# Routing in two halves with 0/1 products for the first expert, and half of the cross-attention's queries made inside its loop

## The chip, the cores and the metric

The kernel runs on one core of a Trainium2 chip, as a program of five engines with queues of their own: TensorE (PE: matmuls and transposes into the 8 banks of PSUM, `ps`), VectorE (DVE), ScalarE (ACT), GpSimd (POOL) and SyncE (SP, which issues most transfers). They are ordered by semaphores alone. The metric is the device time of one execution in microseconds (us).

## What is computed

Sixteen sequences of 64 tokens (T = 1024, width D = 512) pass three blocks, each added to its input after a layer norm. With B = 16, S = 64, NT = 8 tiles of 128 tokens, DC = 4 chunks of 128 features:

```python
x = x + xattn(norm(x), ctx)      # self-attention, cross-attention on 1601 context rows each, MLP of 512
x = x + recurrent(norm(x))       # gates, convolution, linear recurrence of width 768
h = norm(x)                      # then a mixture of 8 experts, 2 for each token, 160 places each
logits = h @ gate_w.T; probs = softmax(logits); top_p, top_i = top_k(probs, 2)
w = top_p / (sum(top_p) + 1e-9)
my_rank = place of the token in the expert's queue (a running count over all tokens)
keep = my_rank < capacity
out = x + sum over the kept (token, expert): w * (silu(h @ Wg[e].T) * (h @ Wu[e].T)) @ Wd[e].T
```

In the cross-attention the keys' matrix is folded into the queries: `m2 = Wq2 @ Wk2.T`, `q = h @ m2` (512 wide), and the scores are `q @ ctx.T`, so that each sequence needs its context twice: by columns (`ctxT`, 3.2 MB) for the scores, and by rows (`ctx`, 3.2 MB) for the values.

## The kernel before

**Order of the dense work.** `dense_groups()` lists every product or transpose that takes a whole PSUM bank; group g has bank g % 8, and it waits until the group 8 places before it has been copied out (`wait_bank_free`). On each engine instructions run in the order written.

**Into the cross-attention.** PE makes the self-attention's `z`, then `m2`, then for each half h of the tokens the four transposes `t1` of its tiles and the four products `q` of 512 columns. ACT copies them out (`hT`, `qT`). DVE meanwhile adds the residual and normalises the eight tiles, computes a decay constant in some 23 tiny steps on 128x6 values (`lac`), waits for all eight `q` copies and clears a piece of PSUM (`pad_cleared`), on which the first scores wait.

**The cross-attention's loop**, for n = 0 to 16 on PE: `scores(n)` (32 matmuls, L508), `transpose_probabilities(n - 1)`, `transpose_output(n - 2)`, `exchange(n)` (tiny products with the counts that DVE made from the scores), `values(n - 1)` (26 matmuls, L532 and L534). Scores of n + 1 need `shifted` of DVE. SP loads the context through two buffers each for columns and rows: the columns of n + 1 once `scores(n - 1)` are done, then the rows of n once `values(n - 2)` are done, in this one order. After the loop come the MLP and the recurrent block, bound to PE.

**Into the experts.** The last dense product `wo` (18 matmuls for a tile) gives the residual; DVE's `residual`, `norm_stats` and `norm_apply` with POOL's `norm_scale` make `hr`, the normalised rows. PE transposes all eight tiles (`t5`) and multiplies them by the gate's weights (`logits`, 8 columns); then, as one chain, DVE makes softmax, top 2 and one-hot (`oh`), PE counts ranks (`rk`), and DVE makes the indices (`scat`). POOL scatters the rows to HBM (`xs`) with 16 indirect transfers, SP waits for all of them and loads the rows of experts 0 and 1 back (`xe`), PE transposes those of expert 0 (`transpose_slots`), and ACT and DVE split them into high and low parts (`xsplit`).

```python
sp.wait_ge(scattered, 16 * NT * TOPK)
load_rows(0, 0)
load_rows(1, 1)
for f in range(RING, FC):
    load_unit(0, f)
```

**The experts.** Each runs 8 units f of weights (768 KB, in a ring of 4, three split ahead): `gate_up` (24 matmuls of 320 columns, L743) and `down` (8 of 512, L759). ACT and DVE split the weights and the hidden values. POOL stores the results, and after the last expert gathers them by `gath` and DVE mixes them in with the routing weights.

## Time and profile before

| | |
|---|---|
| Time, median of 3 runs | 1165.77 us (1164.29 to 1166.39) |
| Profiled execution | 1166.8 us; its span, first to last instruction, 1165.0 us |
| Busy over the span | PE 88%, DVE 49%, ACT 33%, POOL 16% |
| Mean granted TensorE clock | 0.945 |
| Into the cross-attention: first scores start | 150.63 us |
| Cross-attention: last values start | 393.77 us |
| Last `wo` done, first `gate_up` starts | 709.85 us, 773.15 us |

Times in views count from the span's start. A busy PE in a view is modelled from pipelined matmuls, so the pace of a group is read from starts, not from durations. "Idle before" is how long the engine stood before the instruction, with what released it. The clock is 1.00 at 2.4 GHz and 0.50 at 1.2 GHz.

### The profile page before, as it was taken

To read this page: it belongs to the slowest core of one execution; us is meant where nothing else is said; L and a number is where in the kernel's file an instruction comes from. 1 tells how busy PE (TensorE), PEld (TensorE's weight loads), DVE (VectorE), ACT (ScalarE), POOL (GpSimd) and SP (SyncE) were. 2 spreads that over 40 slices of the span, in tenths; PEclk is the share of its full clock that TensorE was granted. 3 is DMA by queue.
4 is the path that set the end of the run, shared out by engine and by line. 5 is a ranking of instruction groups with operands and counts; after the bars stand their busy time and mean duration, and the time that the engine had idled before them with its cause. 6 is when DMAs were issued, how large, how long until landed. Compare 5 with 4: busy or idle time off the path is not lost.

```text
span 1165.0 us, 13668 instructions
## 1 busy us (share of the span) xinstructions
PE 1030.0 (88%) x5132; PEld 760.6 (65%) x5132; DVE 565.7 (49%) x1081; ACT 382.6 (33%) x598; POOL 184.4 (16%) x174
## 2 busy tenths in 40 slices
PE   6999989999988899777999998159999999999970
PEld 3454434444433487665888887159999999999970
DVE  3046523333223287593446664325655655565534
ACT  1211211211111323124566632024444444444420
POOL 2002400000000156243512121500000000000005
PEclk9999999999999999898999997569999999999995
DMA  9724059999999511011411102354545545534306
GB/s 322 320 113 201 25 198 393 418 401 400 401 409 404 204 59 55 1 54 58 129 55 33 35 1 109 117 178 161 184 156 186 180 142 186 195 135 158 131 23 216
DMA packets 38867, 208.04 MB, mean 179 GB/s; under 512 B 5264, under 2 KB 6672, under 8 KB 34592
## 3 DMA queue, kind: packets, MB, share of 16 engines
q1 hardware_dynamic: 33424, 188.47, 43.9%
q0 software_dynamic: 5392, 18.88, 4.6%
q8 instruction: 33, 0.54, 0.2%
q14 instruction: 18, 0.15, 0.0%
HBM read 190.56 MB, written 16.78 MB: 178 GB/s over the span
## 4 chain that ended last, share of the span: by engine, by line
PE 71%; DMA 10%; DVE 8%; issue 6%; POOL 3%; ACT 1%; SPq 0%; POOLq 0%; DVEq 0%; ACTq 0%
PE ps L743 20%; PE ps L573 18%; PE ps L759 10%; PE ps L415 9%; DMA big<-in_ctx 8%; PE ps L532 6%; PE ps L508 5%; DVE stats L1026 1%; POOL big L1568 1%; DVE big L1278 1%; DVE hr L1042 1%; PE ps L729 1%; PE ps L534 1%; DMA big<-in_wk1T 1%; DVE big L1152 1%
## 5 line engine op out<-in xcount | busy, mean ns | idle before, releaser
L743 PE MATMUL ps<-x,w 128*128 128x320 f32 x1536 | 239.2, 312 | 1.0 <-DVE x L1416 1.0
L743 PEld LDWEIGHTS ps<-x,w 128*128 128x128 f32 x1536 | 230.5, 189 | 4.8 <-issue 1.2
L1410 DVE TENSOR_TENSOR w<-big,w 128x1536 fp32r<-128x1536 f32 x64 | 112.4, 1758 | 95.8 <-ACT w L972 95.2
L415 PE MATMUL ps<-big 128*128 128x512 f32 x272 | 121.3, 605 | 12.6 <-DMA big<-in_wk1T 10.6
L759 PE MATMUL ps<-w,hsplit 128*128 128x512 f32 x512 | 128.1, 392 | 0.0
L1499 POOL TENSOR_TENSOR u<-big,u 128x512 fp32r<-128x512 f32 (+1 forms) x44 | 63.8, 1458 | 404.8 <-ACT u L833 404.8
L972 ACT CAST w<-big 128x1536 fp32r<-128x1536 f32 x64 | 94.4, 1478 | 45.5 <-PE ps L759 45.4
L508 PE MATMUL ps<-big 128*64 128x512 f32 (+2 forms) x512 | 100.4, 510 | 9.7 <-DMA big<-in_ctxT 6.4
L759 PEld LDWEIGHTS ps<-w,hsplit 128*128 128x128 f32 x512 | 93.5, 188 | 16.8 <-DVE hsplit L1439 0.3
L415 PEld LDWEIGHTS ps<-big 128*128 128x128 f32 x272 | 52.1, 194 | 76.0 <-issue 65.4
L573 PE MATMUL ps<-xcT,u 128*128 128x512 f32 x432 | 98.1, 389 | 0.0
L573 PEld LDWEIGHTS ps<-xcT,u 128*128 128x128 f32 x432 | 81.1, 188 | 16.8
L532 PE MATMUL ps<-big 128*64 128x512 f32 x384 | 87.6, 606 | 3.3 <-DMA big<-in_ctx 3.3
L573 PE MATMUL ps<-hT,u 128*128 128x512 f32 x288 | 74.2, 421 | 17.3 <-POOL u L1499 10.9
L508 PEld LDWEIGHTS ps<-big 128*64 128x64 f32 x512 | 43.5, 137 | 64.0 <-issue 43.7
L792 ACT COPY big<-ps 128x512 f32<-128x512 f32 (+1 forms) x64 | 32.6, 561 | 148.8 <-PE ps L415 118.2
L573 PEld LDWEIGHTS ps<-hT,u 128*128 128x128 f32 x288 | 58.5, 205 | 32.8 <-POOL u L1499 12.9
L1157 DVE COPY big<-ps 128x512 f32<-128x512 f32 x16 | 11.1, 692 | 129.8 <-PE ps L516 129.8
L997 ACT CAST hsplit<-big 128x320 fp32r<-128x320 f32 x64 | 29.4, 459 | 118.7 <-DVE big L1435 118.7
L1555 POOL DMA_DIRECT2D ys<-big x8 | 5.9, 733 | 363.5 <-DVE big L1426 363.5
L1480 POOL TENSOR_TENSOR rstd<-veps,consts 128x1 f32<-128x1 f32 x48 | 38.7, 808 | 153.3 <-DVE veps L1030 153.3
L532 PEld LDWEIGHTS ps<-big 128*64 128x64 f32 x384 | 26.6, 138 | 51.1 <-issue 47.0
(200 smaller groups left out, 1224.3 us busy)
## 6 DMA issues: line engine op xcount, KB each, us to landing
big<-in_ctxT SPq DMA_DIRECT2D x16, 3202.0 KB, 20.7
big<-in_ctx SPq DMA_DIRECT2D x16, 3072.0 KB
big<-in_w_units SPq DMA_DIRECT2D x64, 768.0 KB, 4.3
big<-in_dense_units SPq DMA_DIRECT2D x42, 256.0 KB, 2.7
xs<-big POOLq DMA_DIRECT2D x1, 5120.0 KB, 25.0
big<-in_gate_units SPq DMA_DIRECT2D x12, 384.0 KB, 3.0
hr<-xs SPq DMA_DIRECT2D x8, 512.0 KB, 5.2
ys<-big POOLq DMA_DIRECT2D x8, 512.0 KB, 3.3
```

The lines of the kernel that those rows point to most:

```text
L415: mm = nc.tensor.matmul(bank(*g)[:, 0:cols], lhsT, rhs, start=(k == 0), stop=(k == len(pairs) - 1))
L508: mm = nc.tensor.matmul(ps[half * S:half * S + S, 2 + piece, 0:w], qT[:, d, n * S:(n + 1) * S], cT[n % 2][:, d, col:col + w], start=(d == ...
L532: mm = nc.tensor.matmul(ps[half * S:half * S + S, 6, :], pts[:, t, half * S:half * S + S], nat[j][:, half * KH + t, :], start=(t == 0), st ...
L573: mm = nc.tensor.matmul(dst, lhs[x], rhs[w], start=start and x + w == 0, stop=stop and x == 1)
L743: mm = nc.tensor.matmul(ps[:, 2 * part + f % 2, 0:SLOTS], wsplit[f % RING][w][:, c:c + P], xsplit[j][x][:, d, :], start=(d == 0 and w + x ...
L759: mm = nc.tensor.matmul(ps[:, 4 + s, :], x, w, start=(f == 0 and k == 0), stop=(f == FC - 1 and k == len(terms) - 1))
L792: signals_evacuated(nc.scalar.copy(dst, src_bank), *g)
L972: nc.scalar.copy(wsplit[f % RING][0][:], wraw[f % RING]).then_inc(w_high, 1)
L997: nc.scalar.copy(hsplit[f % 2][:, 0:SLOTS], hid[f % 2]).then_inc(hid_high, 1)
L1410: V.tensor_tensor(wsplit[f % RING][1][:], wraw[f % RING], wsplit[f % RING][0][:].bitcast(F32), ALU.subtract).then_inc(w_low, 1)
L1480: G.tensor_tensor(rstd[:, i:i + 1], veps[:, i:i + 1], consts[:, 0:1], ALU.pow).then_inc(ln_rstd[L], 1)
L1499: G.tensor_tensor(low[:, 0:w], uraw[u % 4][:, 0:w], high[:, 0:w].bitcast(F32), ALU.subtract).then_inc(u_low, 1)
```

## The change

**Queries.** Only tiles 0 to 3 are transposed (`h2T`) and multiplied (`q`) ahead of the loop. The transposes of tiles 4 to 7 come after `exchange(0)`, their copies on ACT behind `probabilities(0)`, and the four products for the second half come one in each of the iterations 3 to 6, between `exchange` and `values`. The decay constant's steps move into iterations 6 to 14 on DVE. `m2` gets a place of its own.

**Routing.** Tiles 0 to 3 are transposed, given logits and chosen while PE still makes `wo` of tiles 6 and 7; the choice is made on the logits, and the softmax comes later (`route_weights`, in expert 0). Each half has its ranks and indices, and POOL scatters a half when its indices are there. Expert 0's rows don't come from HBM: DVE compares each token's places with the 320 slots (`pick`, 0 or 1), and PE multiplies `hr` by it (`gx`, fp32, 4 chunks by 8 tiles), which gives the rows already transposed. SP loads `xe` for expert 1 after the scatter and after `gx`.

```diff
     g += [("m2", c) for c in range(DC)]
-    for h in range(2):
-        g += [("t1", i) for i in range(4 * h, 4 * h + 4)]
-        g += [("q", c, h) for c in range(DC)]
+    g += [("t1", i) for i in range(4)]
+    g += [("q", c) for c in range(DC)]
...
-    g += [("t5", i) for i in range(NT)]
-    g += [("lg",), ("rk",)]
+    g += [("t5", i) for i in range(4)] + [("lg", 0), ("rk", 0), ("t5", 4), ("lg", 2)]
+    g += [("t5", i) for i in (5, 6, 7)] + [("lg", 1), ("rk", 1)]
+    g += [("gx", d) for d in range(DC)]
...
 SP:
+            load(slot_ids, a["slot_ids"], slots_in)
...
             sp.wait_ge(scattered, 16 * NT * TOPK)
-            load_rows(0, 0)
+            sp.wait_ge(gx_done, 1)
+            sp.wait_ge(xt_done, NS)
             load_rows(1, 1)
...
 PE, in the loop of the cross-attention:
+                    if n == B // 2:
+                        pe.wait_ge(late_q_out, DC)
                     scores(n)
...
                 exchange(n)
+                if n == 0:
+                    late_transposes()
+                if 3 <= n < 3 + DC:
+                    late_queries(n - 3)
                 if n:
                     values(n - 1)
...
 PE, after wo of tiles 0 to 3:
+            for i in (4, 5):
                 for k in range(HC):
                     output_terms(i, k)
+            transposed_tiles(0, 1)
+            for i in range(4):
+                if i < 3:
+                    transposed_tiles(i + 1, i + 2)
+                logits(0, i, 0, 3)
+            for k in range(HC):
+                output_terms(6, k)
+            ranks_within(0)
+            for k in range(HC):
+                output_terms(7, k)
+            transposed_tiles(4, 5)
+            for i in range(4, 7):
+                if i < 6:
+                    transposed_tiles(i + 1, i + 2)
+                logits(1, i, 4, 6)
+            ranks_before()
+            first_expert_rows(0, 0)
+            transposed_tiles(7, 8)
+            first_expert_rows(1, 0)
+            logits(2, 7, 7, 7)
+            first_expert_rows(2, 0)
+            ranks_within(1)
+            first_expert_rows(3, 0)
+            for d in range(DC):
+                first_expert_rows(d, 1)
...
+            def first_expert_rows(d, h):
+                pe.wait_ge(picked, h + 1)
+                if h == 0:
+                    wait_bank_free(pe, "gx", d)
+                for i in range(4 * h, 4 * h + 4):
+                    mm = nc.tensor.matmul(bank("gx", d)[:, 0:SLOTS], hr[:, i, d * P:(d + 1) * P], pick[:, i, :],
+                                          start=(i == 0), stop=(i == NT - 1))
...
-            for s in range(NS):
-                transpose_slots(nth(0, 0), 0, s, first=True)
+            pe.wait_ge(gx_low, 1)
             gate_up(nth(0, 0), 0, 0, first=True)
...
 DVE, after the recurrent block:
+            last_norm(5)
+            last_apply(4)
+            choose(0, 0, 4)
+            last_apply(5)
+            one_hot(0)
+            last_norm(6)
+            positions(0)
+            last_apply(6)
+            last_norm(7)
+            dve.wait_ge(slots_in, 16)
+            pick_rows(0)
+            last_apply(7)
+            choose(1, 4, 7)
+            choose(2, 7, 8)
+            one_hot(1)
+            positions(1)
+            pick_rows(1)
...
+            split_low(0, 0)
+            split_low(0, 1)
+            for d in range(DC):
+                first_expert_low(d)
+            split_low(0, 2)
...
 POOL:
-            pool.wait_ge(idx_done, 2)
-            pool.wait_ge(ln_norm[5], NT)
             pool.wait_ge(xs_zeroed, 16)
             for i in range(NT):
+                pool.wait_ge(ln_norm[5], i + 1)
+                if i % 4 == 0:
+                    pool.wait_ge(idx_done, i // 4 + 1)
```

In `choose`, the eight `V.max` of before and the eight `V.max_index` stay, but those of a half no longer wait one for another. `one_hot` is 3 operations, `positions` 6 to the indices, `pick_rows` one over 128x1280. `first_expert_high` on ACT and `first_expert_low` on DVE are one operation of 320 columns for each chunk. `route_weights` is 10 small operations on DVE, behind unit 1's split in expert 0.

## Rows read from the trace of the kernel before

**Rows 1.** Chain of waits: loop entry and pace, one expert step: start, duration, what.

```profile
135.59 13.98 PE ps L415 x32
150.63 5.81 PE ps L508 x28
...
190.72 5.60 PE ps L508 x27
...
262.95 5.60 PE ps L508 x27
...
812.64 3.52 PE ps L743 x24
```

**Rows 2.** PE timeline, cross-attention: start, duration, line, tiles, idle before.

```profile
160.17 7.26 PE L508 MATMUL ps<-big 128*64 128x512 f32 x32 [2.23 <-DVE s_stat L1175]
...
276.37 1.02 PE L534 MATMUL ps<-big 65*64 65x512 f32 x2
...
384.64 5.37 PE L532 MATMUL ps<-big 128*64 128x512 f32 x24 [0.45 <-DMA big<-in_ctx]
...
390.80 0.98 PE L516 MATMUL ps<-ident,big 128*128 128x128 f32 x7
...
393.77 5.37 PE L532 MATMUL ps<-big 128*64 128x512 f32 x24 [0.79 <-DMA big<-in_ctx]
```

**Rows 3.** 5 us windows: busy PE, PEld, DVE, ACT, POOL; clock; DMA share; GB/s.

```profile
130.00:135.00 5.00, 4.51 (x23) 2.76 (x21) 2.78 (x16) 2.20 (x5) 0.31 (x1) 1.00 0.00 0
...
185.00:190.00 5.00, 5.00 (x26) 1.75 (x24) 3.11 (x12) 1.18 (x3) 0.00 (x0) 1.00 1.01 383
...
715.00:720.00 5.00, 5.00 (x32) 5.00 (x30) 0.00 (x0) 1.76 (x3) 0.00 (x0) 0.61 0.86 354
```

**Rows 4.** SP timeline: issue of the rows of sequence 2's context.

```profile
176.30 0.78 SPq L314 DMA_DIRECT2D big<-in_ctx  x2
```

**Rows 5.** Timeline, about 132 us: transposes and copies of tiles 4 to 7.

```profile
132.60 1.91 PE L422 MATMUL ps<-ident,hr 128*128 128x128 f32 x16
...
132.80 2.54 ACT L792 COPY big<-ps 128x512 f32<-128x512 f32 x5 [2.85 <-PE ps L415]
```

**Rows 6.** PE timeline, end of the recurrent block and logits.

```profile
693.05 0.63 PE L573 MATMUL ps<-u,gh 128*128 128x512 f32 x2
...
709.85 1.03 PE L422 MATMUL ps<-ident,hr 128*128 128x128 f32 x8
...
713.85 0.96 PE L692 MATMUL ps<-gwT,big 128*128 128x8 f32 x8
...
716.69 1.71 PE L692 MATMUL ps<-gwT,big 128*128 128x8 f32 x8
```

**Rows 7.** Timeline, routing and scatter, all engines.

```profile
726.87 0.17 DVE L1377 MAX8 top<-lg 128x8 f32<-128x8 f32 x1
...
730.69 0.17 DVE L1380 CAST rt<-topi 128x16 f32<-128x16 uint32 x1
...
731.83 3.01 PE L709 MATMUL ps<-oh,ones 128*128 128x112 f32 x14
...
737.06 0.17 DVE L1404 CAST scat<-rt 128x16 uint32<-128x16 f32 x1
...
737.61 2.32 POOL L1549 DMA_INDIRECT xs<-hr,scat  x1 [24.88 <-DVE gath L1405]
...
758.67 0.96 POOL L1549 DMA_INDIRECT xs<-hr,scat  x1 [0.30 <-issue]
761.40 2.13 SPq L314 DMA_DIRECT2D hr<-xs  x4
...
773.15 9.12 PE L743 MATMUL ps<-x,w 128*128 128x320 f32 x47 [1.01 <-DVE x L1416]
```

**Rows 8.** Group of the expert weight splits on DVE, 690 to 780 us.

```profile
L1410 DVE TENSOR_TENSOR w<-big,w 128x1536 fp32r<-128x1536 f32 x3 | 5.1, 1749 | 0.0
```

**Rows 9.** The page, DMA issues: size and median us from issue to landing.

```profile
big<-in_w_units SPq DMA_DIRECT2D x64, 768.0 KB, 4.3
```

More of the change, by code:

```diff
@@ L697, in _ @@
-            for i in range(NT):
-                pe.wait_ge(ln_norm[5], i + 1)
-                transpose_rows(("t5", i), hr[:, i, :])
-                if i:
-                    logits(i - 1)
-            logits(NT - 1)
-            pe.wait_ge(oh_done, 1)
-            wait_bank_free(pe, "rk")
-            W = TOPK * NE
-            chosen = oh[:].rearrange("p n e -> p (n e)")
-            for back in range(NT):
-                mm = nc.tensor.matmul(bank("rk")[:, back * W:NT * W], (ones if back else tri)[:],
-                                      chosen[:, 0:(NT - back) * W], start=(back == 0), stop=(back == NT - 1))
@@ L711, in _ @@
-            signals_filled(mm, "rk")
+            transposed_tiles(0, 1)
+            for i in range(4):
+                if i < 3:
[11 more added lines that the diff above has]
+                logits(1, i, 4, 6)
@@ L714, in slots, with transpose_slots @@
+            ranks_before()
[6 more added lines that the diff above has]
+            first_expert_rows(3, 0)
+            for d in range(DC):
+                first_expert_rows(d, 1)
             def slots(s):
                 return P if s < NS - 1 else LAST
-            def transpose_slots(n, j, s, first=False):
+            def transpose_slots(n, j, s):
@@ L718, in transpose_slots @@
                 if s == 0:
                     pe.wait_ge(xe_in[j], n["half"] * 32 + 32)
-                if not (first and s == 0):
-                    pe.wait_ge(xt_low, n["n"] * NS + s)
+                pe.wait_ge(xt_low, n["n"] * NS + s)
                 m = slots(s)
@@ L1008, in _, with first_expert_high @@
                 split_high(0, f, first=True)
-            for s in range(NS):
-                slots_out(0, 0, s)
+            act.wait_ge(rt_shift, 2)
+            nc.scalar.activation(lg[:], lg[:], ACT.Exp).then_inc(rt_exp, 1)
+            nc.scalar.activation(ptop[:], ptop[:], ACT.Exp).then_inc(rt_exp, 1)
+            def first_expert_high(d):
+                act.wait_ge(xt_done if d else gx_done, max(d, 1))
+                nc.scalar.copy(xsplit[0][0][:, d, :], bank("gx", d)[:, 0:SLOTS]).then_inc(xt_high if d else gx_high, 1)
+            for d in range(DC):
+                first_expert_high(d)
             expert(0, 0, first=True)
@@ L1131, in _, with decay_start @@
-            lsteps[0] += 2
-            dve.wait_ge(lac_step, lsteps[0])
-            for k in range(ATANH_TERMS - 2, 0, -1):
+            def decay_start():
+                dve.wait_ge(lac_done, 1)
+                lac_chained(V.tensor_scalar(lac[:, 2, :], lac[:, 1, :], 2.0, None, ALU.add))
+                lac_chained(V.reciprocal(lac[:, 3, :], lac[:, 2, :]))
+                lac_chained(V.tensor_tensor(lac[:, 2, :], lac[:, 1, :], lac[:, 3, :], ALU.mult))
+                V.tensor_tensor(lac[:, 3, :], lac[:, 2, :], lac[:, 2, :], ALU.mult).then_inc(lac_step, 1)
+                V.memset(lac[:, 4, :], 1.0 / (2 * ATANH_TERMS - 1)).then_inc(lac_step, 1)
+                lsteps[0] += 2
+                dve.wait_ge(lac_step, lsteps[0])
@@ L1146, in _ @@
+            for c in range(DC):
+                wait_evacuated(dve, "q", c)
             V.memset(ps[S:P, 3, PIECES[1][2]:PIECES[1][1]], 0.0).then_inc(pad_cleared, 1)
@@ new lines, in pick_rows @@
+            def pick_rows(h):
+                tiles, _ = half_tiles(h)
+                ids = slot_ids.rearrange("p (k s) -> p k s", s=CAP).unsqueeze(1).to_broadcast([P, 4, TOPK, CAP])
+                V.tensor_tensor(pick[:, tiles, :].rearrange("p i (k s) -> p i k s", s=CAP), ids,
+                                r3[4][:, tiles, :].unsqueeze(3).to_broadcast([P, 4, TOPK, CAP]),
+                                ALU.is_equal).then_inc(picked, 1)
+            for i in range(4):
+                last_norm(i)
+                if i:
+                    last_apply(i - 1)
@@ L1444, in expert, with first_expert_low @@
                         split_low(n + (f + AHEAD) // FC, (f + AHEAD) % FC)
+                    if first and f == 1:
+                        route_weights()
                     if f in (2, 4, 5) and not last:
                         slots_low(n + 1, 1 - j, (f - 1) // 2 if f < 5 else 2)
-            for f in range(AHEAD):
-                split_low(0, f)
-            for s in range(NS):
-                slots_low(0, 0, s)
+            def first_expert_low(d):
+                dve.wait_ge(xt_high if d else gx_high, max(d, 1))
+                V.tensor_tensor(xsplit[0][1][:, d, :], bank("gx", d)[:, 0:SLOTS], xsplit[0][0][:, d, :].bitcast(F32),
+                                ALU.subtract).then_inc(xt_low if d else gx_low, 1)
+            split_low(0, 0)
+            split_low(0, 1)
+            for d in range(DC):
+                first_expert_low(d)
+            split_low(0, 2)
             expert(0, 0, first=True)
```

284 lines of the change are left out of this document (177 added, 107 removed).

## The prediction, made before the changed kernel ran

> **What bounds the kernel now.** I read the page first: PE is the busiest engine, so the question is where PE stands still or works alone while something else could. The chain of waits was read second, the timelines of its two weak places third, and windows and groups for prices last.
>
> The first place is the way into the cross-attention and its loop. The chain goes through PE's products right up to the first scores: the second half's `q` runs from 135.59 for 13.98 us, and the scores start at 150.63 [rows 1]. In the windows the reader is to see that the DMA engines stand at 0.00 from 130 to 135, and at 1.01 from 185 to 190 [rows 3]: transfers idle while PE makes queries, and later they are full. Inside the loop PE sets the pace at first: the scores come every (262.95 - 190.72) / 5 = 14.45 us [rows 1]. At the end the last values wait for their context rows [rows 2]. So early the loop is bound by PE, late by the transfers.
>
> The second place is the routing. PE's last `wo` ends at 709.85 and the first `gate_up` starts at 773.15, 63.3 us later [rows 6, 7]. The timeline shows a chain with one engine in each link: transposes and logits, DVE's choice (from before 726.87) and its indices to 737.2, POOL's 16 scatters to 759.6, HBM and back, transposes and splits until 773.15 [rows 7]. From there the experts keep PE full to the end; what is won here moves the end one to one.
>
> **Part 1, the queries.** Removed ahead of the scores: four transposes, their copies and four products. The old first half's products end where the late transposes begin, at 132.60 [rows 5], plus some 0.2 us of pipeline. The way from the last `q` product (135.59 + 13.98 = 149.57) to the first scores (150.63) is 1.06 us, a copy and DVE's clearing [rows 1]. So the scores now start at 132.8 + 1.06 = 133.8: 16.8 us earlier. DVE's `lac` steps no longer stand ahead of the clearing, nor in the way later: in the loop DVE is busy 3.11 of 5 us [rows 3], and two to five steps of about 0.2 us in an iteration lie in the rest.
>
> Added in the loop: 16 transposes (1.91 us, rows 5) after `exchange(0)`. PE stands 2.23 us there, waiting for `shifted` [rows 2], which covers them; without cover they cost 1.9. Their 8 copies on ACT (5 copies of 512 columns took 2.54 us of busy time [rows 5], so 8 of 256 about 3) run under the 7.26 us of `scores(1)` [rows 2]. The four products are 13.98 / 4 = 3.5 us each [rows 1] in iterations 3 to 6, where PE is the bound: they cost 14.0 us of PE time there.
>
> What this gives at the end is set by two bounds. For PE alone: the last two matmuls of values(7) start at 276.37 [rows 2]; seven iterations on it is 377.5, and from there the last iteration, which has no scores, takes 1.0 for these two and 2.2 of small products (390.80 to 393.77, less the wait of 0.79) to the start of the last values: 380.7. They started at 393.77 [rows 2], so 13.1 us went into waits for transfers. After: 380.7 - 16.8 + 14.0 = 377.9, a gain of 15.9. For the transfers alone it is the same train 16.8 us earlier, a gain of 16.8. The two collide in iterations 3 to 6, where a buffer comes free only every 14.45 + 3.5 = 17.95 us. The train at its full rate: from the first rows at 176.30 [rows 4] to the landing at 393.77 [rows 2] are 217.5 us for 14 loads of rows and 12 of columns; a load of rows alone takes 393.77 - 384.64 = 9.1, so a pair of rows and columns (217.5 - 18.2) / 12 = 16.6. Iterations 4 to 6 hold the train up by 17.95 - 16.6 = 1.35 each, 4.1 us (a lead of under 1 us and the delay from issue to transfer I set against each other). Gain: 16.8 - 4.1 = **12.7 us**. Bounds: 15.9 if the train's lead swallows the collision; 8 if it holds it up twice as long.
>
> **Part 2, the routing.** All in before's clock of time, PE first. A `wo` tile costs (709.85 - 693.05) / 4 = 4.2 us [rows 6]; tiles 4 and 5 end at 701.4. Transposes and logits: the third tile's logits began 713.85 - 709.85 = 4.0 us after the first transposes [rows 6], 1.3 a tile; a fourth tile and its logits' end make 5.9 us, to 707.3. DVE then chooses for four tiles. A tile took (730.69 - 726.87) / 8 = 0.48 us [rows 7]; with a copy, one norm and `one_hot` it is done at 710.7, before PE ends `wo` 6 at 711.5. Ranks within the half: 8 instructions at 3.01 / 14 = 0.22 us at the low clock [rows 7], some 1.2 us at the high one; then `wo` 7 to 716.9. DVE's `positions(0)` (6 steps of at most 0.24 us, half of such a choice of two operations) and `pick_rows(0)` lie under this and what follows. Then PE is the chain:
>
> - transposes and logits of tiles 4 to 6: 5.9 - 1.3 = 4.6, to 721.5
> - `ranks_before` 1.2; `first_expert_rows` of one chunk and one half: 4 fp32 products. A product of 512 columns is 2 instructions of 13.98 / 32 = 0.437 us [rows 1]; for 320 columns I take 320 / 512 of it, 0.546 us, so 2.2 us each. Not below that (columns set the pace), and twice that at the low clock
> - four of these, tile 7's transposes 0.6 and logits 0.5, a wait of 0.4 for the bank of `lg` 2, ranks 1.2: to 734.2
> - in the meantime DVE: choice of tile 7, one-hot, `positions(1)` behind the ranks at 732.1 (1.3 us), `pick_rows(1)`. That is 1280 columns against 1749 ns for 1536 [rows 8], 1.5 us: done 735.0, 0.9 us after PE came free
> - four chunks of the second half, 8.75 us, to 743.8; a cast of 320 columns on ACT and a subtraction on DVE, estimated at 0.5 each from the same 1749 ns by columns and a fixed part, with 0.4 of signals: `gate_up` at **745.3**.
>
> ACT and DVE have split the first weights by then (3 and 2 casts of up to 1.75 us [rows 8] between 726 and 739). Against 773.15 this is 27.9 us. The clock comes on top, both ways. Before, it fell to 0.50 in the logits (mean 0.61 over 715 to 720 [rows 3]): the same 8 instructions took 0.96 us at 713.85 and 1.71 at 716.69 [rows 6], about 6 us after the dense products stopped, and `gate_up`'s first 47 instructions took 9.12 us [rows 7], where 24 take 3.52 at the high clock [rows 1], so 6.9: the gain is 2.2 more, as PE is now dense ahead of `gate_up`. But the two new stretches of transposes and logits (5.9 and 4.6 us long) can each bring a fall, of which one cost about 1.7 us (gate_up lost 2.2): 3.4 us. Sum for part 2: 27.9 + 2.2 - 3.4 = **26.7 us**. Bounds 20 (falls twice as long, 3.4, and DVE late by 3.3) and 30.1 (no fall).
>
> On the clock, the Trainium skill (TensorE: Matmul & The Clock Gate, Part 4) says that transposes don't count as PE work to the gate, and the fall among back-to-back transposes and 8-column products agrees. By it both stretches would bring a fall, which is the charge I made; without it the sum would be 30.1.
>
> **The scatter.** It no longer stands ahead of expert 0, but SP waits for it before expert 1's rows and, behind them, units 4 to 7 of expert 0. POOL's scatters follow `norm_scale` of tile 7: the first eight from 719.8, the second eight from 733.6. At 1.27 us each (0.96 and 0.30, rows 7) the last is issued by 743.8; 1.8 us to SP's go (759.6 to 761.40), 2.1 of issuing [rows 7], 4.3 for a unit to land [rows 9] and 1 more beside other transfers: unit 4 is there near 753. It is needed on ACT at about 756 (`gate_up(4)` runs near 765), so it is hidden by 3 us. `route_weights`, 10 steps of some 0.2, comes on DVE in the same unit and fits below the 1.8 us by which `down` trails the split; at worst 1 us.
>
> **Sum.** 12.7 + 26.7 = 39.4 us off the profiled 1165.0 of span: 1125.6, and 1127.4 with the 1.8 around it. The median of the runs is 1.0 below the profiled time, so **1126.4 us**.
>
> **The rivals.**
> - No fall of the clock and no collision: 15.9 + 30.1 = 46.0 off, 1120. For it: the first stretch lies between dense products. Against it: the clock fell after such a stretch [rows 6]. 12%.
> - The clock stays low through the 0/1 products. From 716.9 the work of 28.4 us would be about 24 longer, `gate_up` near 770, its own start still slow; gain 3, with part 1 1150. Against it: fp32 products of 512 columns ran at the high clock for 14 us [rows 1]. 9%.
> - The loop gives nothing, since each late product delays a buffer by more than computed: 1139. 7%.
> - The scatter becomes the bound. The issue took 2.32 us at 737.61 while DVE split weights, 0.96 after [rows 7]; now DVE works beside nearly all of them. At 2.62 us each the last is issued at 762 and unit 4 lands near 771, 15 us late: 1141. 7%.
> - Slower than before by the same mechanism: it decides when the issue costs over 4.1 us each (719.8 + 16 x 4.1 + 9.2 is 39 us past 756, as much as the forecast gains). No row shows more than 2.32. 2%, and 1% for no change.
>
> The Trainium skill (SBUF — State Buffer, Who interferes with whom) has this as its rule: POOL and DVE share a port pair, and a copy, cast or tensor_scalar of DVE in its two-port mode shuts POOL out while it runs. By it the first eight scatters would stretch to the 15 us case. The trace shows only tensor_tensor beside a scatter, with the 2.32 us at its worst.
>
> **How the numbers follow.** The forecast as computed has 62%; its own range is 1121 to 1134. The cases on the faster side sum to 97%; one of these I leave to what I don't see, so 96, 1 and 3%. Within 0.2% is what a measurement of this kernel can't tell from no change. The range for 8 in 10 takes in the better case and the 1139: 1117 to 1139.
>
> **What would show it.** First scores near 133.8; scores every 18 us in iterations 3 to 6; waits for context gone before sequence 13 or so; last values starting near 381. Last `wo` to first `gate_up` 28 to 32 us; the 16 fp32 products of the second half in 8.8 us; unit 4's cast never waited for. Wrong would be: a low clock at the 0/1 products, PE's waits for context rows as many as before, or ACT's L972 waiting for `w_units`.

## The result, and the profile after

The changed kernel takes 1119.93 us (median of 4 runs, 1116.04 to 1121.53), the kernel before 1165.14 beside it (4 runs, 1164.29 to 1166.39): a ratio of 0.9621, 95% interval 0.9587 to 0.9654. The forecast was 1126.4. The profiled execution took 1121.53, its span is 1119.5 us, 45.5 less than before's 1165.0; the mean granted clock is 0.973 (before 0.945). On the three other chips single runs of before lay between 1158 and 1167, so a few us between two medians of one series say little.

Cut at four landmarks, the 45.5 us are: last values of the cross-attention 393.77 to 378.34, 15.4; from there to the end of `wo` of tile 5, 307.7 to 304.8, 2.9; from that to the first `gate_up`, 71.7 to 45.7, 26.0; the experts, 391.8 to 390.7, 1.2. (Tile 5 of before ended at 709.85 less two tiles of 4.2, 701.45.)

The chain of waits of the changed kernel: the scores of sequences 0, 3 and 4 with a late product between them, the last free-running scores, and the one transfer in it. It answers to [rows 1].

```profile
132.98 5.81 PE ps L536 x28
...
171.59 5.60 PE ps L536 x27
179.88 3.54 PE ps L520 x8
189.57 5.60 PE ps L536 x27
...
345.14 5.60 PE ps L536 x29
360.05 18.24 DMA big<-in_ctx
```

The scores start 17.65 us earlier than in [rows 1]. From 171.59 to 189.57 are 17.98 us with a late product, of 3.54. Inside the loop a DMA stands in the chain once, at its very end. Over the whole chain, in the page, PE rose to 81% (before 71), DMA fell to 3% (before 10).

```profile
PE 81%; DVE 10%; POOL 3%; DMA 3%; issue 1%; ACT 1%; POOLq 0%; SPq 0%; DVEq 0%; ACTq 0%
```

PE's timeline of the changed kernel in the cross-attention, answering to [rows 2].

```profile
140.15 1.94 PE L511 MATMUL ps<-ident,hr 128*128 128x128 f32 x16
142.51 5.78 PE L536 MATMUL ps<-big 128*64 128x512 f32 x32 [0.42 <-DVE s_stat L1281]
...
360.85 5.81 PE L536 MATMUL ps<-big 128*64 128x512 f32 x32 [1.20 <-DMA big<-in_ctxT]
...
369.65 5.37 PE L562 MATMUL ps<-big 128*64 128x512 f32 x24 [0.23 <-DMA big<-in_ctx]
...
378.34 5.37 PE L562 MATMUL ps<-big 128*64 128x512 f32 x24 [0.35 <-DMA big<-in_ctx]
```

The 16 late transposes fill what was 2.23 us of waiting for `shifted`; 0.42 is left. The scores after them take 5.78 us where before took 7.26 for the same 32 instructions. PE waits for context only from the scores of sequence 15 on, 1.8 us in all; before it waited from the scores of sequence 9 on.

The queue of SP, the rows of sequence 2, answering to [rows 4].

```profile
157.17 0.78 SPq L321 DMA_DIRECT2D big<-in_ctx  x2
```

The routing of the changed kernel on all engines, a selection of lines, answering to [rows 6, 7] (L433 transposes, L721 logits, L609 `wo`, L825 `gate_up`, L1523 `pick_rows`, L759 the 0/1 products, L1649 `norm_scale`, L1719 the scatter, L1064 ACT's cast of weights).

```profile
683.10 1.04 PE L433 MATMUL ps<-ident,hr 128*128 128x128 f32 x8
687.04 3.10 PE L721 MATMUL ps<-gwT,big 128*128 128x8 f32 x16
690.00 1.20 PE L609 MATMUL ps<-u,gh 128*128 128x512 f32 x2
693.98 0.73 PE L609 MATMUL ps<-u,gh 128*128 128x512 f32 x2
701.27 1.03 PE L433 MATMUL ps<-ident,hr 128*128 128x128 f32 x8
703.37 1.73 POOL L1649 TENSOR_TENSOR rstd<-veps,consts 128x1 f32<-128x1 f32 x1 [4.46 <-DVE veps L1133]
703.93 1.90 PE L721 MATMUL ps<-gwT,big 128*128 128x8 f32 x16
705.27 1.09 POOL L1719 DMA_INDIRECT xs<-hr,scat  x1 [0.18 <-issue]
706.60 2.37 PE L759 MATMUL ps<-big,hr 128*128 128x320 f32 x8
717.27 1.48 DVE L1523 TENSOR_TENSOR big<-big,rt 128x1280 f32<-128x1280 f32 x1
718.13 1.45 POOL L1719 DMA_INDIRECT xs<-hr,scat  x1 [2.92 <-DVE scat L1518]
718.80 8.88 PE L759 MATMUL ps<-big,hr 128*128 128x320 f32 x32 [0.59 <-DVE big L1523]
719.89 1.59 POOL L1719 DMA_INDIRECT xs<-hr,scat  x1 [0.30 <-issue]
728.51 0.96 POOL L1719 DMA_INDIRECT xs<-hr,scat  x1 [0.30 <-issue]
728.82 7.27 PE L825 MATMUL ps<-x,w 128*128 128x320 f32 x48 [1.13 <-DVE x L1613]
731.23 0.98 SPq L321 DMA_DIRECT2D hr<-xs  x2
738.61 1.48 ACT L1064 CAST w<-big 128x1536 fp32r<-128x1536 f32 x1 [0.95 <-DMA big<-in_w_units]
```

Before, PE stood 31.29 us for the rows from HBM:

```profile
766.13 1.08 PE L729 MATMUL ps<-ident,hr 128*128 128x128 f32 x4 [31.29 <-DMA hr<-xs]
```

Now it waits 0.59 for `pick_rows` and 1.13 for the last split. The 16 logits at 687.04 take 3.10, the same 16 at 703.93 take 1.90: the clock was low from about 687 to 694, and the first `wo` products of tile 6 (690.00, 1.20 for two) ran slowly too. `gate_up` starts at the high clock: 48 instructions in 7.27, against 47 in 9.12 [rows 7]. The scatters run from 705.27 to 729.5, mostly under PE's work, and the cast of unit 4 waits 0.95 for its transfer; PE does not wait behind it.

### The profile page after: what moved, and what is told of

It reads as the page before. It is cut to its first block, busy times and chain, and to the rows that moved or that the text cites. A ratio compares the mean times of both kernels' runs of the same rounds, so it can differ in the third digit from the quotient of the medians.

```text
span 1119.5 us, 13822 instructions
## 1 busy us (share of the span) xinstructions
PE 1033.4 (92%) x5191; PEld 763.7 (68%) x5191; DVE 562.7 (50%) x1093; ACT 382.2 (34%) x604; POOL 185.6 (17%) x174
## 4 chain that ended last, share of the span: by engine, by line
PE 81%; DVE 10%; POOL 3%; DMA 3%; issue 1%; ACT 1%; POOLq 0%; SPq 0%; DVEq 0%; ACTq 0%
PE ps L825 20%; PE ps L609 19%; PE ps L841 11%; PE ps L426 8%; PE ps L536 8%; PE ps L562 7%; DMA big<-in_ctx 2%; PE ps L759 1%; POOL big L1739 1%; DVE big L1258 1%; PE ps L520 1%; DVE stats L1128 1%; DVE big L1391 1%; PE ps L564 1%; PE ps L433 1%
## 5 line engine op out<-in xcount | busy, mean ns | idle before, releaser
L825 PE MATMUL ps<-x,w 128*128 128x320 f32 x1536 | 237.2, 311 | 1.1 <-DVE x L1613 1.1
L825 PEld LDWEIGHTS ps<-x,w 128*128 128x128 f32 x1536 | 228.5, 188 | 5.3 <-issue 1.6
L426 PE MATMUL ps<-big 128*128 128x512 f32 x240 | 106.8, 605 | 11.2 <-DMA big<-in_wk1T 10.4
L1064 ACT CAST w<-big 128x1536 fp32r<-128x1536 f32 x64 | 94.4, 1478 | 43.9 <-PE ps L841 42.9
L536 PE MATMUL ps<-big 128*64 128x512 f32 (+2 forms) x512 | 102.9, 505 | 2.7 <-DMA big<-in_ctxT 1.2
L609 PE MATMUL ps<-xcT,u 128*128 128x512 f32 x432 | 98.1, 389 | 0.0
L609 PEld LDWEIGHTS ps<-xcT,u 128*128 128x128 f32 x432 | 81.1, 188 | 16.8
L426 PEld LDWEIGHTS ps<-big 128*128 128x128 f32 x240 | 46.0, 194 | 66.8 <-issue 56.4
L609 PE MATMUL ps<-hT,u 128*128 128x512 f32 x288 | 74.1, 421 | 17.4 <-POOL u L1668 10.9
L609 PEld LDWEIGHTS ps<-hT,u 128*128 128x128 f32 x288 | 58.5, 205 | 32.8 <-POOL u L1668 12.9
L872 ACT COPY big<-ps 128x512 f32<-128x512 f32 (+1 forms) x56 | 28.2, 556 | 141.5 <-PE ps L426 104.9
L1649 POOL TENSOR_TENSOR rstd<-veps,consts 128x1 f32<-128x1 f32 x48 | 39.4, 822 | 160.1 <-DVE veps L1133 160.1
## 6 DMA issues: line engine op xcount, KB each, us to landing
big<-in_ctxT SPq DMA_DIRECT2D x16, 3202.0 KB, 14.5
```

What stands on the lines that cost most here:

```text
L426: mm = nc.tensor.matmul(bank(*g)[:, 0:cols], lhsT, rhs, start=(k == 0), stop=(k == len(pairs) - 1))
L536: mm = nc.tensor.matmul(ps[half * S:half * S + S, 2 + piece, 0:w], qT[:, d, n * S:(n + 1) * S], cT[n % 2][:, d, col:col + w], start=(d == ...
L609: mm = nc.tensor.matmul(dst, lhs[x], rhs[w], start=start and x + w == 0, stop=stop and x == 1)
L825: mm = nc.tensor.matmul(ps[:, 2 * part + f % 2, 0:SLOTS], wsplit[f % RING][w][:, c:c + P], xsplit[j][x][:, d, :], start=(d == 0 and w + x ...
L872: signals_evacuated(nc.scalar.copy(dst, src_bank), *g)
L1064: nc.scalar.copy(wsplit[f % RING][0][:], wraw[f % RING]).then_inc(w_high, 1)
```

## Experiments

Each is told with before's time in the same series; the later two series hold the changed kernel itself again, as a control.

**Each half of the change alone.** `e1_queries` has only the queries' part, `e2_routing` only the routing's (the hunks of the diff above that carry the other part are undone).

```diff
 e1_queries, on before:
-    for h in range(2):
-        g += [("t1", i) for i in range(4 * h, 4 * h + 4)]
-        g += [("q", c, h) for c in range(DC)]
+    g += [("t1", i) for i in range(4)]
+    g += [("q", c) for c in range(DC)]
 e2_routing, on before:
-    g += [("t5", i) for i in range(NT)]
-    g += [("lg",), ("rk",)]
+    g += [("t5", i) for i in range(4)] + [("lg", 0), ("rk", 0), ("t5", 4), ("lg", 2)]
```

> The queries' part alone, on the kernel before (first half ahead of the loop, second half inside it, the decay's steps inside it too; routing as before). Theory A, that the two parts touch different stages and add: in the changed kernel the last values start 14.6 us earlier than before when the difference at the loop's entry is taken off, and another 1 to 2.6 us come back behind the loop, where the clock rose sooner; so 15 to 17 us off, near 1149 us, and last values near 378. Theory B, the sum as predicted, with the transfers held up in iterations 3 to 6: 12.7 off, near 1152.5. Theory C, that the routing's part changed something here: neither.

> The routing's part alone, on the kernel before. Theory A (parts add): first gate_up 26 us earlier than before and its start 2 us shorter, 27 to 28 us off, near 1137.5. Rival, that the halves only pay when the clock is as it was in the changed kernel: up to 3.4 us less or more, 1134 to 1141, with the falls of the granted clock at other places than there.

Beside before at 1160.66 us: queries alone 1147.84, ratio 0.9882 (0.9844 to 0.9920); routing alone 1135.94, ratio 0.9769 (0.9730 to 0.9808). Together 3.49% of before's time, the whole change 3.79%: the two parts add up within the intervals. In the traces the last values start at 378.79 with the queries' part and at 392.39 without it (before 393.77); from the last `wo` to `gate_up` are 60.4 us without the routing's part (691.46 to 751.88) and 29.2 with it (714.26 to 743.50). The median of the queries' part is 12.8 us under before's, with an interval of 9 to 18, so it can't tell its theories A (15 to 17) and B (12.7) apart; the last values, 15.0 us earlier than in before, speak for A. The routing's median is 24.7 us under, where 27 to 28 were expected, with an interval of 22 to 31.

The two traces also show a thing that the forecast had not in it. PE's timeline of routing alone shows the scores of sequence 1 behind the wait of 2.23 us that before has:

```profile
149.01 5.78 PE L517 MATMUL ps<-big 128*64 128x512 f32 x32 [1.06 <-DVE ps L1208]
158.55 8.34 PE L517 MATMUL ps<-big 128*64 128x512 f32 x32 [2.23 <-DVE s_stat L1237]
```

In windows of 5 us (columns as in [rows 3]) before ran these scores at a mean clock of 0.68:

```profile
160.00:165.00 5.00, 4.83 (x16) 1.75 (x18) 0.17 (x3) 1.08 (x2) 0.00 (x0) 0.68 1.05 449
```

and the changed kernel did not:

```profile
140.00:145.00 5.00, 4.58 (x30) 2.94 (x32) 2.13 (x7) 2.41 (x8) 0.00 (x0) 1.00 0.85 348
```

With the queries' part alone they took 5.78 us, and so they did in each of the other eleven traces of kernels that have this part. So in both traces without it the clock fell here, around a wait of 2.23 us, and in the twelve with it, where transposes fill most of that wait, it did not. Before lost 7.26 - 5.78 = 1.5 us by it. What else the clock needs in order to stay up is not shown by this pair.

**A quarter of each late product.** Only the first of the four chunks of each of the second half's query products is done, so that the queries of sequences 8 to 15 lack three quarters of their terms; 10.5 us of PE's work go out of iterations 3 to 6.

```diff
-                for d in range(DC):
-                    mm = nc.tensor.matmul(ps[:, 1, :], m2[:, d, tok(c)], late2T[d], start=(d == 0), stop=(d == DC - 1))
+                mm = nc.tensor.matmul(ps[:, 1, :], m2[:, 0, tok(c)], late2T[0], start=True, stop=True)
```

> The changed kernel, where each late product does one of its four chunks (3.5 us of PE in all instead of 14; the queries of sequences 8 to 15 are then not the reference's). Theory A, that PE is the bound of the loop up to sequence 14 and the transfers are only just behind: the transfers' own bound takes over at once, so that of the 10.5 us taken off PE only 2 to 2.5 come back, near 1117.5, and waits for context return from sequence 8 on. Theory B, the predicted collision of 4.1 us: 3 to 4 us come back. Theory C, that the transfers have slack in the changed kernel: 6 us or more come back, near 1113.

Measured 1117.87 us beside 1160.66, ratio 0.9624 (0.9581 to 0.9668), not to be told from the whole change. In the trace, from the first scores to the last values are 240.4 us, against 245.4 in the changed kernel: 5.0 of the 10.5 come back, more than theory B had and less than C. PE waits for context from the scores of sequence 12 on (theory A had 8), and these come at the transfers' pace, (340.12 - 307.34) / 2 = 16.4 us:

```profile
307.34 5.81 PE L535 MATMUL ps<-big 128*64 128x512 f32 x32 [1.19 <-DMA big<-in_ctxT]
...
323.82 5.81 PE L535 MATMUL ps<-big 128*64 128x512 f32 x32 [1.20 <-DMA big<-in_ctxT]
...
340.12 5.81 PE L535 MATMUL ps<-big 128*64 128x512 f32 x32 [1.22 <-DMA big<-in_ctxT]
```

**Each late product twice.** The second time overwrites the first.

```diff
-                for d in range(DC):
-                    mm = nc.tensor.matmul(ps[:, 1, :], m2[:, d, tok(c)], late2T[d], start=(d == 0), stop=(d == DC - 1))
+                for again in range(2):
+                    for d in range(DC):
+                        mm = nc.tensor.matmul(ps[:, 1, :], m2[:, d, tok(c)], late2T[d], start=(d == 0), stop=(d == DC - 1))
```

> Each product of the second half's queries within the cross-attention is done twice (the first result is overwritten by the second, so nothing of the output changes): four more products of 3.54 us, 14.2 us of TensorE in iterations 3 to 6. Theory A, the loop runs at TensorE's pace up to its last iterations: the last values come 12.4 to 14.2 us later (14.2 less the 1.9 that TensorE waits for the context in the last three iterations) and the time rises by the same. Theory B, half of what TensorE does there is hidden behind the context's transfers (as the run with a quarter of the products suggested, 10.5 us less work for 5.0 less loop): the last values come about 7 us later. The measured slope on the other side of zero tells which step the forecast's hold-up term was.

Measured 1135.27 us, the control beside it 1122.17: 13.1 more. In the trace the late iterations take 21.42 us instead of 17.98, 13.8 in all, and from the first scores to the last values are 258.3 us against 244.6 in the control, 13.6 more. So work added to the loop costs all of itself, and work taken out gives back half: the changed kernel stands just on PE's side of the point where transfers and PE cost the same. PE's waits for context at the end are 0.83 us in all, against 1.23 in the control:

```profile
373.16 5.81 PE L537 MATMUL ps<-big 128*64 128x512 f32 x32 [0.59 <-DMA big<-in_ctxT]
```

The transfers show where they are held up. In windows of 5 us from 185 to 260 the DMA share never falls below 0.92 with a quarter of the products. In the changed kernel it dips three times, to 0.76 (205 to 210), 0.78 (225 to 230) and 0.83 (240 to 245), behind the second to fourth late product. With twice the products it dips four times, to 0.45, 0.31, 0.20 and 0.42.

**Halves without 0/1 products.** The routing in halves, but expert 0's rows through HBM as before.

```diff
 SP:
+            load_rows(0, 0)
             load_rows(1, 1)
...
 PE (the other first_expert_rows, and pick_rows on DVE, go as well):
-            for d in range(DC):
-                first_expert_rows(d, 1)
...
+            for s in range(NS):
+                transpose_slots(nth(0, 0), 0, s, first=True)
             gate_up(nth(0, 0), 0, 0, first=True)
```

> The changed kernel without the 0/1 products: routing in halves, but expert 0's rows are scattered, loaded back and transposed as before. The last scatter was issued 729.5 us into the span of the changed kernel, and its issue depends on indices that come some 6 us earlier without products between the ranks: near 724. Landing 1.8, rows back 4.7, transposes and splits 7.2: first gate_up near 738 instead of 728.8. Theory A (the products are worth what the round trip costs past the last index): 9 us slower than the changed kernel plus 2 for the low clock at gate_up's start, near 1131. Rival, that halves alone give nearly all: less than 4 us slower. Rival, that the 0/1 products give nearly all: 20 us slower or more.

Measured 1132.49 us beside 1160.66, ratio 0.9746 (0.9698 to 0.9794). PE's timeline:

```profile
707.29 1.87 PE L720 MATMUL ps<-gwT,big 128*128 128x8 f32 x8 [0.68 <-ACT big L869]
...
732.37 1.09 PE L805 MATMUL ps<-ident,hr 128*128 128x128 f32 x4 [20.06 <-DMA hr<-xs]
...
739.39 5.85 PE L819 MATMUL ps<-x,w 128*128 128x320 f32 x22 [1.01 <-DVE x L1571]
```

`gate_up` starts 10.6 us later than in the changed kernel, its first 48 products take 9.66 against 7.27, as in before: 12.7 us of span in all. From `wo` of tile 5 to `gate_up` are 56.9 us, where before has 71.7 and the changed kernel 45.7. So the halves give 14.8 of the routing's 26 us, and the 0/1 products 11.2 and the 2.4 of the low clock at `gate_up`'s start. That low clock has a visible beginning: it fell at 707, under tile 7's transposes and logits (707.29: 1.87 us for 8 logits that otherwise take 0.95), and stayed low through PE's wait of 20.06 us.

**The first half not scattered early.** POOL waits for the second half's indices before any scatter.

```diff
-                    pool.wait_ge(idx_done, i // 4 + 1)
+                    pool.wait_ge(idx_done, 2)
```

> The changed kernel, where POOL scatters nothing before the second half's indices are there, so that the last scatter is issued some 10 us later (near 739 us of the span instead of 729.5). Theory A, that the scatter is hidden with about 3 us to spare and unit 4 of expert 0 is what comes late next: ACT waits some 9 us at unit 4's cast (0.95 in the changed kernel), and PE stands 4 to 5 us in expert 0: 4 to 5 us slower. Theory B, that the experts' ring of weights hides all of it: no difference. Theory C, that the scatter sets the start of the experts: 10 us slower.

Measured 1132.43 us, the changed kernel beside it 1119.48 (its control `c0_after_again`, below): 13.0 slower, where 4 to 5 were expected. `gate_up` starts at 727.18, in the control at 727.43. SP issues the rows 14.6 us after that (741.74), in the control 2.4 us after it (729.86): 12.1 us later. From `gate_up` to the end are 401.4 us, in the control 391.0, so 10.4 of them come out. A selection of lines:

```profile
745.98 1.12 PE L811 MATMUL ps<-ident,hr 128*128 128x128 f32 x4 [4.33 <-DMA hr<-xs]
746.75 5.95 PE L825 MATMUL ps<-x,w 128*128 128x320 f32 x24
748.53 1.47 ACT L1064 CAST w<-big 128x1536 fp32r<-128x1536 f32 x1 [12.51 <-DMA big<-in_w_units]
755.41 3.49 PE L841 MATMUL ps<-w,hsplit 128*128 128x512 f32 x8 [2.71 <-DVE hsplit L1600]
```

Two waits of PE, 4.33 for expert 1's rows and 2.71 for work on ACT and DVE that stands behind unit 4's cast, and a low clock after each: 5.95 us for 24 products that otherwise take 3.76, 3.49 for 8 that take 2.0. The two waits are 7.0 us together, so some 5 of the 12.1 us are hidden; the low clock behind the waits gives most of that back. What I had missed in the expectation is that the clock follows a wait, and that `transpose_slots` of expert 1 stands in PE's order inside expert 0.

**The same, with units 4 and 5 of the weights issued ahead of SP's wait.**

```diff
+            for f in range(RING, RING + 2):
+                load_unit(0, f)
             sp.wait_ge(scattered, 16 * NT * TOPK)
...
-            for f in range(RING, FC):
+            for f in range(RING + 2, FC):
                 load_unit(0, f)
```

> The run in which nothing is scattered before the second half's indices, with the last two weight units of expert 0 issued ahead of the wait for the scatter on the queue, so that only the rows stand behind it. Theory A, of the 13 us that the late scatter cost, most is the wait for those weights (12.5 us of ScalarE's idle time): the time comes to within 4 to 6 us of the changed kernel, and what stays is TensorE's wait for expert 1's rows (4.3 us). Theory B, the rows' lateness costs it all by itself (a wait, then a low clock behind it): it stays 10 us or more slower.

Measured 1126.80 us beside the control's 1122.17: 4.6 slower. ACT's 12.51 us are gone, PE's wait for the rows is 2.62, with no low clock behind it, and from `gate_up` to the end are 394.5 us (control 391.6):

```profile
746.04 0.66 PE L813 MATMUL ps<-ident,hr 128*128 128x128 f32 x4 [2.62 <-DMA hr<-xs]
```

So of the 10.4 us after `gate_up` in the trace of the late scatter, 2.9 are the rows', and the rest is that of the weights queued behind them, with the clock.

**The changed kernel again, and the first half's transposes spread out.** `c0_after_again` and `d0_after_third` are the changed kernel itself. `c1_interleaved` puts the transposes and logits of tiles 0 to 3 one by one between the steps of `wo` of tiles 5 and 6, so that there is no stretch of them; in `c2_tile7_first` tile 7's transposes, logits and ranks come one group of products earlier as well.

```diff
 c1_interleaved:
...
+            wo_steps(5, 3, 4)
+            transposed_tiles(1, 2)
+            wo_steps(5, 4, 5)
+            logits(0, 0, 0, 3)
+            wo_steps(5, 5, 6)
...
 c2_tile7_first, on c1_interleaved:
-            first_expert_rows(0, 0)
             transposed_tiles(7, 8)
-            first_expert_rows(1, 0)
+            first_expert_rows(0, 0)
             logits(2, 7, 7, 7)
-            first_expert_rows(2, 0)
+            first_expert_rows(1, 0)
             ranks_within(1)
+            first_expert_rows(2, 0)
```

> The changed kernel once more, unaltered, as the measure for the three beside it on the same chip: 1116 to 1122 us. In its first trace the granted clock is low 20.5 us in all between the loop and the last wo tile (27.3 in the kernel before) and once, for 6.8 us, after the first four tiles' transposes and logits. If these falls depend on the work, the second fall comes again at the same place; if they are chance, they move.

> The changed kernel itself, as the measure for the three beside it. Expected 1117 to 1121 us. Whether the granted clock falls in the first stretch of transposes and logits of the last projection is open: it did in two of the two executions profiled so far of this very kernel; with the fall the last stretch from the gate's transposed weights to the last matmul of the last tile takes some 16.7 us, without it 13.5.

> The changed kernel with the transposes and logits of tiles 0 to 3 put one by one between the wo steps of tiles 5 and 6 instead of in one stretch. Theory A, that the stretch of sparse PE work makes the clock fall: no fall at this place, so 3.4 us less, and 1.2 us of waits for ACT's copies less: 4 to 5 us faster than the changed kernel. Theory B, that the clock falls there whatever the order: 1 to 1.5 us faster.

> The same as c1_interleaved, and tile 7's transposes and logits and the second ranks each one 0/1 product group (2.2 us) earlier. In the changed kernel PE waited 0.4 us for a bank, some 0.4 for the second one-hot's ranks' order and 0.6 for the second pick. Theory A, that PE's own work is the chain and only its waits can go: 1 us faster than c1. Theory B, that DVE's chain from tile 7's logits to the second pick is the chain: 2.2 us faster. Rival: nothing, since DVE is then late with tile 7's norm.

Before 1161.42 beside the first three: the changed kernel 1119.48, ratio 0.9632 (0.9607 to 0.9658); spread out 1118.90, 0.9639 (0.9612 to 0.9667), the same; tile 7 first 1116.57, 0.9613 (0.9587 to 0.9638). In the third series the changed kernel took 1122.17 beside 1163.51, 0.9643 (0.9619 to 0.9666), 1.2 us above what was expected.

The second trace of the changed kernel has the fall of the clock in the first stretch once more. The third has not: its windows show it in the second stretch instead, going over into the 0/1 products, with the same instructions in the same order:

```profile
685.00:690.00 5.00, 5.00 (x27) 4.21 (x28) 2.30 (x18) 0.00 (x0) 0.00 (x0) 1.00 0.00 0
...
700.00:705.00 5.00, 5.00 (x18) 3.37 (x17) 0.40 (x5) 0.39 (x1) 3.85 (x4) 0.66 0.99 343
```

From the first logits to the end of `wo` 7 are 16.9 us with the fall in the first stretch (the changed kernel's first two traces) and 13.8 without it (the third), so a fall there costs 3.1 us. A fall in the second stretch makes the way from the last `wo` to `gate_up` 29.2 us instead of 27.6 (the routing alone, the late scatter), 1.7 us. Over all runs with the two stretches in the changed kernel's order there are nine traces: five have a fall in the first stretch, the other four in the second. Eight have this one fall only; the ninth, the one without 0/1 products, has a fall in the first and a second one at 707. The three kernels with the first four tiles spread out have none, in the second stretch neither, though that one is unchanged.

Spread out, the work from the end of `wo` of tile 4 to `gate_up` takes 46.4 us (678.91 to 725.28), against 49.9 in the changed kernel's first two traces (678.90 to 728.82 in the first), 3.5 us less. The medians over five rounds don't show that (0.6 apart, with intervals of some 3 us on either side), so the 4 to 5 us of theory A are not shown in the time; in the trace the fall of the clock at this place is gone, as that theory had it.

Tile 7 first shortens the way from the last `wo` to `gate_up` to 26.1 us, from 27.6 in the kernel beside it: `pick_rows` is done in time, and 48 instructions of 0/1 products follow without a gap. These 1.5 us lie between the theories' 1 and 2.2.

```profile
710.17 13.17 PE L759 MATMUL ps<-big,hr 128*128 128x320 f32 x48
724.47 5.80 PE L836 MATMUL ps<-x,w 128*128 128x320 f32 x38 [1.13 <-DVE x L1624]
```

**Tile 7 first, and units 4 and 5 ahead of SP's wait.** The edit is the one above, on `c2_tile7_first`.

> The order with tile 7's transposes and logits first (1.4 us shorter from the last tile to gate_up), and units 4 and 5 of expert 0 issued ahead of the wait for the scatter. If the 0.95 us that ScalarE waited for unit 4 is all that this takes away, nothing more comes of it, since TensorE did not wait there: 1115 to 1118 us, 2 to 3 under the changed kernel. If the rows of expert 1, now behind more weights on the queue, come late, it is 2 to 4 us slower than that.

Measured 1118.11 us, ratio 0.9609 (0.9582 to 0.9635), beside the control's 1122.17 and 0.9643. The unit's cast is not waited for in either of the two kernels with tile 7 first (ACT's wait there ends with PE, 0.37 and 0.36 us), so the weights' earlier issue had nothing to remove. In this trace DVE stood 4.43 us before the second ranks although PE had made them 3.5 us earlier, which moved the second half's products 1.8 us back:

```profile
713.54 0.23 DVE L1523 TENSOR_TENSOR rk<-ps,oh 128x64 f32<-128x64 f32 x1 [4.43 <-remote]
```

What held it is not in the trace. In both series the kernel with tile 7 first is ahead of the changed one, by 2.9 and 4.1 us of median (0.3%), but the intervals of the ratios overlap each time; it is the version to take, with a gain that is likely and not shown.

## Why the prediction was right, and by what its terms were off

The forecast was 39.4 us off the span, measured are 45.5, and the median is 6.5 us below the forecast. The mechanisms that carry the sum stood. One thing that was named as a sign of being wrong came in a small size: ACT's cast of unit 4 waited for `w_units`. The sizes add up as follows: 2.7 us more in the loop, 2.9 behind it, 1.6 more in the routing, 1.0 less in the experts.

- **First scores**, forecast 133.8: 132.98. PE's last `q` product ended at 131.95 instead of 132.8; the way from there took 1.03, forecast 1.06.
- **Late transposes hidden in the 2.23 us**: right, and they gave more than nothing. The term left out is the low clock on the scores after this wait, 7.26 us against 5.78, 1.5 us. It stood in [rows 2], where I took the 7.26 only as a cover for ACT's copies.
- **Four products of 3.5 us, scores every 18 us**: 3.54 and 17.98.
- **Loop gain, "16.8 - 4.1 = 12.7"**: the last values came 15.4 us earlier. The train of transfers started 176.30 - 157.17 = 19.1 us earlier, and took from there 221.2 instead of 217.5 us: held up by 3.7, forecast 4.1. Over all traces the train takes 219.6 to 222.1 us in the ten with whole late products, 216.2 to 217.5 in the three with a quarter of them or none: 4.0 between the means. So the collision was sized right, and what was off is the "same train 16.8 us earlier": it ran 2.3 us ahead of that, by the earlier start and the clock above. 0.85 + 1.5 + 0.4 is the 2.7 us that were missed. The run with a quarter of the products, whose train took 373.60 - 157.41 = 216.2 us, shows that the 217.5 are the transfers' own, to 1.3; the run with twice as many, that PE pays for all that is added. That run also bounds the forecast's formula. Three iterations held up by 21.42 - 16.6 us would be 14.5, measured are some 17.3 (a train of 234.1 us): there all four hold the train up, while in the changed kernel the train's lead took in the first.
- **From the last values to `wo` of tile 5**, forecast unchanged: 2.9 us less. Its products are as they were; the third trace of the changed kernel took 302.3 us for it, where the first took 304.8. The granted clock goes with it: summed over the windows of this stretch it was low for 27.3 us in before (307.7 us long), for 20.5 in the first trace of the changed kernel (304.8), and for 17.0 in the third (302.3). The same program differs by 2.5 us here, so the 2.9 are in part chance, and why the clock was low for less is open.
- **Routing, 43.9 us from `wo` 5 to `gate_up` and 3.4 for two falls of the clock, 47.3**: measured 45.7. One fall came instead of two, and cost 3.1 where 1.7 were charged, since it ran on into `wo` of tile 6: two errors that nearly cancel, which is luck. A first-half chunk took 2.2, as forecast; the second half's products 8.88 (8.75); the split and signals behind them 1.13 us as the last wait. `pick_rows` took 1.48 (1.5), PE waited 0.59 for it (0.9). What is left, 1.3 us, lies in small steps, such as ranks before (0.92 for 1.2) and transposes. From the last `wo` to `gate_up` are 27.6 us, just under the 28 to 32 that were given as a sign.
- **`gate_up` at the high clock, 2.2 us**: 7.27 for 48 against 9.12 for 47, 2.0. But from `gate_up` to the end only 1.2 us are gained; where the other 0.8 went is open.
- **The scatter, "hidden by 3 us"**: it was hidden from PE, and not from ACT, whose cast of unit 4 waited 0.95 us (0.98 and 0.42 in the other two traces). "Unit 4's cast never waited for" was wrong. The last scatter ended at 729.5, where the forecast, moved by `gate_up`'s own 16.5 us, has 727.3; and ACT was ready for the unit at 737.7, where the forecast, so moved, has 739.5. The late scatter shows what was left for PE: of 12.1 us of delay it waited 7.0, and lost most of the other 5 to the clock.

Of the rivals, the one at 1120 (no fall of the clock and no collision) has the measured number but not the mechanism: the clock fell once, and the train was held up. The slow 0/1 products did not come: the second half's 32 took 8.88 in the changed kernel's three traces. The one first chunk that a fall met in them took 4.03 us instead of 2.37, in the third. The scatter as a bound did not come either; the issues beside `pick_rows` and the first splits took 1.45, 1.59 and 1.36 us, the next ones 0.96, among them the last, which had a split of weights beside it too (DVE from 728.59).

Of the two rules of the Trainium skill one says that transposes don't count as PE work to the clock gate (TensorE: Matmul & The Clock Gate, Part 4), which would put a fall into both stretches. The traces bear it out in part: all nine with this order have a fall, eight of them in only one of the two stretches, and with the first stretch broken up there was none in the second either. The loop's entry speaks against it: there 16 transposes in place of a wait kept the clock up, in twelve traces of twelve. The other says that DVE's two-port operations shut POOL out (SBUF — State Buffer, Who interferes with whom). The one scatter beside a `tensor_scalar` took 1.09 us with that operation 0.60 long, which is small here. The same section says that a `tensor_tensor` with both inputs in SBUF contends with POOL's reads, which the prediction left out. Three issues beside such operations took 0.4 to 0.6 us more than alone, and one took no more.

## What to carry to other kernels

When a loop is bound by its engine early and by its transfers late, work moved into it is paid in part up to the point where both take the same time, and in full beyond it: here the first 10.5 us cost 5.0, and 13.8 more cost 13.6. Compute both ends of the loop, and look for the first transfer's issue, since the train's start is what moves. A wait in PE's order has a price beyond itself when the next instructions run at the low clock; compare an instruction group's duration with the same group elsewhere before taking it as given. And where a queue waits for rows, look at what is queued behind them: of the 13.0 us that the late scatter cost, all but 4.6 went when the weights were taken out from behind it.

## What the runs showed of the hardware that was not expected

- The same program had its fall of the clock in the first stretch of transposes and logits in two executions, and in the second stretch in a third one (685 to 690 at 1.00, 700 to 705 at 0.66). A single trace can't say where an order has its fall, and its price differs by the place, 3.1 us or 1.7. That a change of the first stretch alone took the fall out of the second too was not foreseen, and three traces show it.
- In the two kernels in which PE waits 2.23 us at the loop's start the clock fell within this wait and was low behind it; with 16 transposes and 0.42 us of wait in its place it stayed at 1.00, in twelve traces.
- `norm_scale` of POOL, a `tensor_tensor` on one column, took 1.73 us beside DVE's `pick_rows` (two operands in SBUF, 1280 columns, 1.48 us), and 0.55 beside small operations of at most 64 columns (tile 6): it started 0.17 us after `pick_rows` and ended 0.4 after it.
